# Token tiles of an attention and FFN layer transposed by transfers instead of TensorE, on eight cores

## What is computed

```python
def attn(x):                      # 16 heads of 64
    q = x @ Wq + bq
    k = (x @ Wk + bk) @ Wl + bl
    v = (x @ Wv + bv) @ Wl + bl
    o = softmax(q @ k.T / 8) @ v  # per head
    return o @ Wo + bo

def ffn(x):
    base = x @ base_W.T + base_b
    shared = (x @ shared_A.T) @ shared_B.T             # rank 16
    gate = softmax(x @ router_W.T + router_b)          # 6 experts
    w = top2(gate) / (sum(top2(gate)) + 1e-6)
    routed = sum_e w_e * ((x @ routed_A[e].T) @ routed_B[e].T)
    return base + shared + routed

x = x + LN(attn(LN(x)))
x = x + LN(ffn(LN(x)))
```

## Time and profile before

| | us |
|---|---|
| median of 3 runs | 1417.14 |
| lowest, highest | 1416.58, 1481.97 |
| profiled execution, its time | 1416.75 |
| its span on the slowest core (core 5) | 1415.2 |
| spans of the 8 cores | 1410.1 to 1415.2 |
| mean granted TensorE clock of the cores | 0.987 to 0.990 |

### The profile page before, as it was taken

One profiled execution on the slowest core, in us unless ns is written; L12 is line 12 of the kernel. 1 busy time (PEld: TensorE's weight loads), 2 busy tenths in 40 slices (PEclk: granted clock), 3 DMA queues, 4 the chain that ended last, 5 costly groups with the idle time before them and its releaser, 6 DMA issues.

```text
span 1415.2 us, 43939 instructions; the slowest of 8 cores (1410.1 to 1415.2 us)
## 1 busy us (share of the span) xinstructions
PE 1319.1 (93%) x17392; PEld 818.9 (58%) x17392; DVE 703.6 (50%) x1679; ACT 1042.2 (74%) x1138; POOL 428.1 (30%) x590
## 2 busy tenths in 40 slices
PE   4999999999999999999988999989999999999883
PEld 1456666666666576665645555655555555556551
DVE  0552443323333323232224666676767766667666
ACT  0457777777777777777767888887888788887651
POOL 3220111000000101000004555554565555555633
PEclk9999999999999999999999999999999999999998
DMA  9950112202020210123842122312213221212011
GB/s 139 238 147 6 54 30 73 65 19 56 15 62 20 50 38 26 24 80 64 123 112 79 54 76 77 120 40 91 76 45 115 76 74 56 91 69 76 32 62 45
DMA packets 65977, 98.90 MB, mean 70 GB/s; under 512 B 30080, under 2 KB 41728, under 8 KB 65264
## 3 DMA queue, kind: packets, MB, share of 16 engines
q1 hardware_dynamic: 56656, 81.99, 18.3%
q0 software_dynamic: 8832, 13.06, 6.6%
q10 hardware_dynamic: 288, 1.05, 0.2%
HBM read 76.56 MB, written 32.57 MB: 77 GB/s over the span
## 4 chain that ended last, share of the span: by engine, by line
PE 79%; DVE 7%; issue 5%; ACT 4%; DMA 2%; POOL 2%; DVEq 0%; ACTq 0%; POOLq 0%
PE fb L377 35%; PE sc L1117 17%; PE av L1149 15%; ACT p_sb L1134 4%; PE fb L429 4%; PE sc L377 2%; DMA wl_sb<-wl 2%; DVE gt L891 1%; DVE x L807 1%; PE fb L848 1%; PE fb L771 1%; PE av L377 1%; PE sc L1119 1%; DMA bb_t<-rows 1%; PE fb L322 1%
## 5 line engine op out<-in xcount | busy, mean ns | idle before, releaser
L1134 ACT ACTIVATE p_sb<-sc 128x1024 bf16<-128x1024 f32 x1024 | 991.0, 1021 | 267.7 <-PE sc L1119 264.7
L1149 PEld LDWEIGHTS av<-v_sb,p_sb 128*128 128x128 bf16 x8192 | 321.7, 98 | 97.0 <-issue 2.5
L1117 PE MATMUL sc<-q_sb,k_sb 64*128 64x256 bf16 (+1 forms) x2176 | 331.4, 266 | 15.8 <-ACT p_sb L1134 14.4
L1149 PE MATMUL av<-v_sb,p_sb 128*128 128x65 bf16 x8192 | 340.6, 193 | 0.0
L1119 PE MATMUL sc<-q_sb,k_sb 64*128 64x256 bf16 (+1 forms) x2176 | 333.6, 267 | 0.6 <-issue 0.6
L1117 PEld LDWEIGHTS sc<-q_sb,k_sb 64*128 64x128 bf16 x2176 | 150.0, 94 | 83.5 <-issue 47.4
L264 POOL TENSOR_SCALAR rsa<-sta 128x1 f32<-128x1 f32 x32 | 7.2, 226 | 527.8 <-DVE sta L259 392.7
L1119 PEld LDWEIGHTS sc<-q_sb,k_sb 64*128 64x128 bf16 x2176 | 146.6, 94 | 0.0
L377 PE MATMUL fb<-wo_sb,ut 128*128 128x512 bf16 x496 | 137.1, 383 | 4.9 <-DVE gt L885 3.7
L377 PE MATMUL fb<-bw_sb,x3fm 128*128 128x512 bf16 x480 | 136.0, 384 | 1.0 <-DVE x3fm L249 0.9
L377 PE MATMUL fb<-xfm,wq_sb 128*128 128x512 bf16 x512 | 129.5, 381 | 0.0
(11 more groups left out here) (178 smaller groups left out, 1466.5 us busy)
## 6 DMA issues: line engine op xcount, KB each, us to landing
xst<-x SPq DMA_DIRECT2D x64, 512.0 KB, 4.8
out<-y_sb SPq DMA_DIRECT2D x31, 512.0 KB, 3.0
urow<-u_scr SPq DMA_DIRECT2D x30, 256.0 KB, 4.8
u_scr<-u SPq DMA_DIRECT2D x64, 64.0 KB, 2.2
q_scr<-kq SPq DMA_DIRECT2D x32, 128.0 KB, 2.1
q_sb<-q_scr SPq DMA_DIRECT2D x4, 1024.0 KB, 8.1
u_scr<-u_sb SPq DMA_DIRECT2D x7, 512.0 KB, 3.2
wkT_sb<-wkT POOLq DMA_DIRECT2D x8, 256.0 KB, 14.3
```

Source lines behind the costliest of these rows:

```text
L1117: t.matmul(sc[slot][:, ci * w:(ci + 1) * w], k_sb[0:64, j, c * 128:(c + 1) * 128], qa[0:64], start=True, stop=True, tile_position=(0, 0))
L1134: exp_tok[g] = P.op("S", lambda a: a.activation(ps[:], sc[slot][:], AF.Exp, bias=-SHIFT, scale=1.0), tok, av_tok.get(g - 4))
L1149: r = t.matmul(av[u % 2][:, o:o + 65], ps[:, p0:p0 + 128], v_sb[:, j, c * 130 + h * 65:c * 130 + (h + 1) * 65], start=(s == 0 and h == 0 a ...
```

## The change

A DMA that transposes (`dma_start(..., transpose=True)`), issued from SP, takes the place of TensorE's transposes and of DVE's copies out of PSUM for three kinds of tiles: sequence 1's input (16 tiles), the attention's output (30 of 32) and the normalised rows of the FFN (30 of 32). Each tile is 8 DMAs of one 128x128 block (`dma_blocks`). The two `urow` buffers go, `ut` has four buffers instead of two, and `load_u` fills `ut` straight from DRAM. The load of x, which was in `tr_u`, is `load_r`. Sequence 1's input and the normalised rows are transposed from SBUF to SBUF. In the plan these items cost 0 in place of 2.0, `h_group(n-1)` stands five products later and is held for 3 steps of the clock behind `tr3` instead of 1, and z's first half for 3 steps behind `load_u`. Sequence 0's input and the last two tiles stay as they were.

```diff
+    def dma_blocks(self, e, sem, out, in_, *toks):
+        self.wait(e, *toks)
+        for c in range(NCH):
+            sem[1] += 16
+            self.q[e].append(lambda eng, o=out[:, c, :], i=in_[:, c * 128:(c + 1) * 128], h=sem[0]:
+                             eng.dma_start(out=o, in_=i, transpose=True).then_inc(h, 16))
+        return (sem, sem[1])
...
-        urow = [at("urow%d" % i, X0 + 28544 + 2048 * i, [D], BF16) for i in range(2)]
+        ut = [at("ut%d" % i, X0 + 28544 + 2048 * i, [NCH, 128], BF16) for i in range(2)]
...
-        ut = [at("ut%d" % i, X1 + 8192 + 2048 * i, [NCH, 128], BF16) for i in range(2)]
+        ut += [at("ut%d" % (2 + i), X1 + 8192 + 2048 * i, [NCH, 128], BF16) for i in range(2)]
...
         def tr_in(n, f, tt):
+            if not state["p0"]:
+                xs = xn_slot[n]
+                tok = P.dma_blocks("Y", qxf[4 * (f - 4) + tt], xfm[f][:, :, tt * 128:(tt + 1) * 128], xn[xs], xn_tok[n],
+                                   xfm_free[f])
+                xn_free[xs] = tok
+                xfm_tok.setdefault(f, {})[tt] = tok
+                return
...
-                    qs[i] = within(qs[i], (2.0, lambda t=t, tt=tt, f=f: tr_in(ln_of[1, t], 9 - f, tt), None))
+                    qs[i] = within(qs[i], (0.0, lambda t=t, tt=tt, f=f: tr_in(ln_of[1, t], 9 - f, tt), None))
...
         def load_u(n):
-            if n < NSEQ * 16 - 2:
-                seq, t = tile_of(n)
-                done_at(("l", n))
-                u_ld[n] = P.dma("Y", qur[n % 2], urow[n % 2][:], u_scr[seq, t], u_tok[n // 2][1],
-                                urow_free[n % 2], fb_tok["a1"])
+            seq, t = tile_of(n)
+            done_at(("l", n))
+            ut_tok[n] = P.dma_blocks("Y", qur[n % 4], ut[n % 4], u_scr[seq, t], u_tok[n // 2][1],
+                                     u_free[n % 4], fb_tok["a1"])
+
+        def load_r(n):
+            res[n] = load_x(*tile_of(n))
...
         def tr3(n):
             s = n % 2
+            if n < NT - 2:
+                done_at(("t", n))
+                x3_tok[n] = P.dma_blocks("Y", qx3[s], x3fm[s], xn3[s], xn3_tok[n], x3_free[s], fb_tok["a1"])
+                xn3_free[s] = x3_tok[n]
+                return
...
-            return [(2.0, lambda: tr3(n), past(("x", n), 3))]
+            return [(0.0 if n < NT - 2 else 2.0, lambda: tr3(n), past(("x", n), 3))]
...
-            return held(h_group(n), past(("t", n), 1))
+            return held(h_group(n), past(("t", n), 3 if n < NT - 2 else 1))
...
-            tu = [(2.0, lambda n=n: tr_u(n + 1), past(("l", n + 1), 2))] if n + 1 < NT - 2 else []
-            z0 = held(z_group(n, 0), past(("u", n), 1))
+            tu = [(0.0, lambda n=n: load_r(n + 1), None)] if n + 1 < NT - 2 else []
+            z0 = held(z_group(n, 0), past(("l", n), 3))
...
-                filler += y0[:2] + th_of(n - 2) + y0[2:6] + h + y0[6:] + y1[:4] + (tu if late(n + 1) else [])
+                filler += y0[:2] + th_of(n - 2) + y0[2:] + y1[:2] + h + y1[2:4] + (tu if late(n + 1) else [])
```

More of the change, by code:

```diff
@@ L199, in build_nc @@
         qus = [P.new("qus%d" % i) for i in range(2)]
-        qur = [P.new("qur%d" % i) for i in range(2)]
+        qur = [P.new("qur%d" % i) for i in range(4)]
+        qxf = [P.new("qxf%d" % i) for i in range(8)]
+        qx3 = [P.new("qx3_%d" % i) for i in range(2)]
         qy = [P.new("qy%d" % i) for i in range(2)]
@@ L639, in build_nc @@
         ones = []
-        first = [(2.0, lambda tt=tt: tr_in(ln_of[1, tt], 4, tt), None) for tt in range(4)]
+        first = [(0.0, lambda tt=tt: tr_in(ln_of[1, tt], 4, tt), None) for tt in range(4)]
         def within(group, item, at=4):
@@ L703, in build_nc @@
         u_last = {}
-        u_free = [None, None]
+        u_free = [None] * 4
         ut_tok = {}
@@ L740, in tile_of @@
             return n // 16, n % 16
-        u_ld = {}
-        urow_free = [None, None]
         def u_ready(n):
@@ L751, in load_u @@
         def load_u(n):
-            if n < NSEQ * 16 - 2:
-                seq, t = tile_of(n)
-                done_at(("l", n))
-                u_ld[n] = P.dma("Y", qur[n % 2], urow[n % 2][:], u_scr[seq, t], u_tok[n // 2][1],
-                                urow_free[n % 2], fb_tok["a1"])
-        def tr_u(n):
[L761 to L765, removed]
+            seq, t = tile_of(n)
[4 more added lines that the diff above has]
+            res[n] = load_x(*tile_of(n))
+        def tr_u(n):
+            load_r(n)
             b = next_bank()
@@ L770, in mm @@
                 for c in range(NCH):
-                    r = e.transpose(pb[:, c * 128:(c + 1) * 128], src[:, c * 128:(c + 1) * 128], identb[:])
-                return r
[L773 to L776, removed]
+                    r = e.transpose(pb[:, c * 128:(c + 1) * 128],
+                                    u_sb[1][:, n % 2, c * 128:(c + 1) * 128], identb[:])
+                return r
+            tok = P.op("T", mm, u_last[n][0], bfree[b])
+            done_at(("l", n))
+            ut_tok[n] = ev_copy("V", ut[n % 4][:], pb.rearrange("p (c t) -> p c t", c=NCH), tok, u_free[n % 4],
                                 fb_tok["a1"])
@@ L802, in z_group @@
         def z_group(n, h):
-            s, xs = n % 2, n % 4
+            s, xs = n % 4, n % 4
             def evict(pa, tok):
@@ L961, in build_nc @@
         filler += bo_quanta()
-        add(lambda: tr_u(0), 2.0, past(("l", 0), 2))
+        add(lambda: load_r(0))
         def late(n):
@@ L1020, in build_nc @@
         gates(a, 0)
-        z0 = held(z_group(c, 0), past(("u", c), 1))
+        z0 = held(z_group(c, 0), past(("l", c), 1))
         filler += z0[:4] + t3_of(b) + z0[4:]
@@ L1253, in build_nc @@
         last_tile()
-        for sem in [qc, *qw.values(), *qrow, *qx, *qkq, *qvo, *qql, *qkl, *qvl, *qu0, *qus, *qur, *qy]:
+        for sem in [qc, *qw.values(), *qrow, *qx, *qkq, *qvo, *qql, *qkl, *qvl, *qu0, *qus, *qur, *qxf, *qx3, *qy]:
             P.wait("Y", (sem, sem[1]))
```

## The result

Before 1417.14 us, after 1981.57 us (medians of five runs each); the lowest run after is 1926.94 us. The ratio is 1.361, interval 1.358 to 1.364: the kernel is 36% slower. The ratio is less than that of the medians because it leaves out runs in which the cores of one die ran longer at a lower clock; the profiled execution (span 1925.4 us) is not one of those. The sign was forecast and so was the place; the size was not: 1509.5 us, with a range up to 1785.

A forecast was written before the change was run, and what follows sets the result against it. TensorE was taken to bound the kernel before, a loop through SP's queue after. The terms -7.2 - 2.7 + 102.6 = +92.7 us gave 1509.5 us from 1416.75; range 1378 to 1785, likeliest case 1443 to 1597.

The forecast's parts named there:

- the chain h, y, POOL, store of `out`, SP, x3, h: Second half's FFN tiles: a loop closing once per tile through SP's queue, 24.5 us in place of 20.7.
- What d is: Step estimating SP's time d to issue one transposing DMA, from other issues on SP: 0.60 us taken.
- the prediction's own formula: Period of an FFN tile in the second half: 14.9 + 16 d, from 12.1 + 0.97 + 1.8 + 16 d.
- The high end: Upper bound for d on SP: 1.2 us each for two q loads of 1 MB.
- rival C: Transposing transfers on SP don't overlap, each keeping the path about its own time: period 34.1 us, 1775 us; chance 16%.
- the low end: Lower bound for d on SP: a copy is never under 0.32 us, u stores take 0.37 at the median.
- The legs ahead of the store: Second half, from h's start through DVE, TensorE and POOL to the store of `out`: 12.1 us.
- The 9.3 us of cover: Sequence 0's half: time from a slab's last input transpose to first use, said to cover the 6.6 us needed.
- A gain of 7.2 us: Sequence 0's half: 16 tiles of input transposes leave TensorE, 0.45 us each, with transfers covered.
- TensorE's gain: Second half, per FFN tile: 0.9 us of transposes and 1.0 of bank waits go, 20.7 to 18.8 us for TensorE alone.
- A: Rival: issues as fast as a short copy, or a shorter chain on SP; 1356 to 1388 us, value 1375; chance 19%.
- B: Rival: about even, TensorE's savings return as waits, d 0.33 to 0.44; 1393 to 1439 us, 1415 middle; chance 15%.

The follow-up runs named there:

- the part with x3 only: Against the kernel before, only the FFN's normalised rows are transposed by DMA: 1632.84 us, ratio 1.153; with the store of `out` behind these transposes, 1441.04 us.
- the part alone: Against the kernel before, only sequence 1's input is transposed by DMA, u and x3 staying on TensorE: 1441.87 us, ratio 1.018.
- the last run above: The whole change with one DMA per tile, x3's transfer ahead of the store of `out` and u's transfer on SP: 1400.33 us, ratio 0.9885 against the kernel before.

## Why the prediction was right and where it was wrong

**The bound and the loop: right.** The prediction named the chain h, y, POOL, store of `out`, SP, x3, h as what would set the tile's time, and TensorE's idle time before the small product as its sign. The waits are there, 449.5 us in 30, though 15 us each and not 4 to 6, and the order on SP alone takes 192 us off the part with x3 only (1632.84 to 1441.04).

**What d is: wrong, and this step carries the miss.** "What d is" took 0.60 us from the nearest copies; a transposing DMA holds SP for 1.23 us, 1.32 from one to the next with what lies between. Those for x3 from 900 to 1700 us, as far as recorded (ns min/median/max):

```profile
L76 SPq DMA_TRANSPOSE x3fm<-xn x173: 1093/1232/1237, 899.2 to 1699.7; - x173
```

In the prediction's own formula 1.32 gives 14.9 + 21.1 = 36.0 us, and 37.9 were measured; the paragraph on the legs has the rest. The high end from the rows of before, 1.2 us per q load, came within 0.03 us of the hold, and stood as rival C. But C was told as transfers that don't overlap, with a chance of 16%. That mechanism did not occur, since a block lands 2.3 us after its issue starts and the next is issued after 1.23. Its price nearly did: 1775 us was C's value, and the fastest run took 1926.94. The reason given for the low end, that a transposing issue can't be quicker than a copy, said nothing on how much slower it is, and the nearest row was taken as if it did.

The Trainium skill's 1309 ns for a 128x128 transpose by DMA ("VectorE: DVE Perf Modes", The three transpose paths), weighed as C's neighbour, is close to the hold of 1232 ns; what the runs add is that it belongs to the instruction and not to the 128x128 block. The Trainium skill's rule that transposing DMAs are as fast as ordinary ones ("Advanced Engine Details and Errata", X-Bar Transpose) does not hold here for one block of 32 KB: its issue takes 1.23 us against 0.33 for a copy, and it lands after 2.3 us against 1.8.

**The legs ahead of the store: 12.1 said, 14.3 measured.** Three products of y1 take 1.46 us behind h (the 1325.15 line) where the three ahead of the last one (from 1327.96) take 0.82, and y's last product ends 6.6 us after h starts, not 4.5. The granted clock is 0.50 in the 5 us behind the wait, so TensorE's first work after it, which is in the loop, runs slower: h itself takes 0.94 us against 0.60. The prediction called this an end of the range, not a term. Against that, the landing was 1.4 us behind the last issue and not 1.8. The formula with both is 36.0 + 2.2 - 0.4 = 37.8 us.

**The landing in front of TensorE in sequence 0's half: wrong sign.** The 9.3 us of cover were compared with 6.6; with the measured hold 8 x 1.32 + 1.1 = 11.7 are needed, and what is ahead on SP comes on top. The longest wait, 14.3 of the 22.7 us, is for the first slab, which the prediction did not count (it took three slabs). In the kernel before, that slab's last transposes start at 195.22 us and its first product at 201.75. After, SP starts that tile's transposes only at 202.98, since POOL had waited 14.9 us, in two tiles, for the transposes ahead to free `xn`. A gain of 7.2 us was booked; the part alone costs 25. With one DMA per tile the waits are gone and the first store is 7.6 us early, so the gain is there once the issues are few. In the whole change the first store is 53 us late: 22.7 us are these waits, and 5.5 for u and 24.8 for x3 follow in the first output tiles; less the 7.2 saved that is 46, and the other 7 were not separated. The rest of the difference to before is 22 x 17.2 = 378 us in the regular tiles and 79 behind them.

**TensorE's gain: too large.** 1.9 us per tile were said, 0.9 of transposes and 1.0 of waits for a bank. Where nothing else is late (the last run above) the tile gains 0.8. Of the 26.1 us that were read as waits for a bank, put 15.4 down to "issue", a time in which the engine waited for nothing that the profile shows; only 10.7 were waits for DVE. And of these a part moved to the next small user of a bank, the transpose of the expert input (line 941): it waits for the same evictions, 8.3 us in 12 times, where it was 3.4 in 6 before.

**The rivals.** A, a gain in the regular tiles, needs a loop under the 20.7 us of before; it took one instruction per tile and another order on SP, and brought 1.1%. B, no change, did not come.

## What to carry to other kernels

Before work is moved to DMAs, count the instructions that the issuing queue must take per round, with the price of that kind of DMA and not of a copy, and follow what stands ahead of the first one that somebody needs: a store that waits for the end of the round, put ahead of the next round's inputs, ties the rounds into a loop. Transpose as much per DMA as one instruction takes, and issue what is needed soon ahead of what waits long. When an operation has no row in the trace, a far row is no centre; give its high end the chance that it deserves, or measure it alone first.

## What the runs showed of the hardware

A transposing DMA (bf16) holds the issuing sequencer for 1.21 us at 16x128, 1.23 at 128x128 and 1.33 at 128x1024, from DRAM or SBUF, and some 1.26 from ACT; a plain copy of 32 KB holds SP for 0.33. It lands 2.3 us after its issue starts, 3.2 for 128x1024 from SBUF, and 5.1 right behind a 512 KB store, a 512 KB load and another transposing DMA. The DMA engines were not the limit in the regular tiles: busy 0.14 to 0.24 in the change, 0.32 to 0.39 in the fastest kernel. TensorE's granted clock in a stretch followed its waits: 0.74 to 0.81 with 15 us of waiting in a tile, 0.83 to 0.90 with x3 alone (6 us), 1.00 where no such wait was left. In the 5 us right behind a wait of 16.8 us it was 0.50.
